# Rank 2 in place of rank 3 for the expert blocks of the second layer, in a one-core kernel of four gated layers

## The chip, the cores and the metric

The kernel runs on one core of one Trainium2 chip. The metric is device time in microseconds (us) from the first to the last instruction of the core; lower is better. A core has five engines that run side by side, each through its own list of instructions in order: PE (TensorE, matmuls), DVE (VectorE), ACT (ScalarE), POOL (GpSimd) and SP (SyncE, which here only issues transfers). They wait for each other by semaphores alone, so an instruction that waits holds up all that stand behind it on its engine.

## The reference

The input `x` has 32 sequences of 128 tokens with 128 features. It passes four layers, each a gated attention followed by a gated feed-forward part:

```python
x = x + tanh(g_xattn[0]) * L0_xattn(ctx, layernorm(x), b, seq_len)     # 16 heads
x = x + tanh(g_ffn[0])   * L0_ffn(layernorm(x), ...)                   # dense, 128 -> 512 -> 512 -> 512 -> 128
x = x + tanh(g_xattn[1]) * L1_xattn(layernorm(x), ctx, ...)            # 16 heads
x = x + tanh(g_ffn[1])   * L1_ffn(layernorm(x), ...)                   # see below
x = x + tanh(g_xattn[2]) * L2_xattn(ctx, layernorm(x), mask, b)        # 8 heads
x = x + tanh(g_ffn[2])   * L2_ffn(layernorm(x), ...)                   # 8 experts, top 2
x = x + tanh(g_xattn[3]) * L3_xattn(layernorm(x), ctx, ...)
x = x + tanh(g_ffn[3])   * L3_ffn(layernorm(x), ...)
```

The change lies in `L1_ffn` and in the attention behind it. `L1_ffn` is itself a causal attention with a mixture of experts behind it:

```python
h = rmsnorm(x, g1); c = h @ w_down
q, k, v = rope(c @ wq), rope(c @ wk), c @ wv           # 16 heads of 4
x = x + causal_softmax(q k^T / 2) v @ w_up
t = rmsnorm(x, g2); probs = softmax(t @ router_w)      # 8 experts
gate = the two largest probs of each token, scaled to sum 1
y = sum over experts of gate * (silu(t @ w1) * (t @ w3)) @ w2
```

## The kernel before

**A plan first, then five programs.** `make_plan` (from line 344 on) writes one long list of steps in Python. `run_program` then goes through that list once for each engine, and each engine emits its own part of every step. The order of the list is therefore the order of instructions on every engine. The plan keeps a clock for each engine with a reckoned cost for each kind of step (`reckon`), and uses it only to decide which piece comes next.

**Main work and side work.** An attention phase goes through 32 sequences (`b0` to `b31`). A step `scores` is a score tile for DVE to find row maxima in, `weights` is the transposed tile for ACT to take the exponential of, `sums` the product with the values. `weights` of a sequence come `lag` sequences after its `scores` (4 where there are 8 heads, 2 with 16). Everything else is side work: units with a need (semaphore counts that must be reached by the plan's clock) and a rank. `soon` puts a unit into the list `side` behind all units of the same or a lower rank number. `run_side(n, rank)` takes, up to n times, the first unit whose rank is at most `rank` and whose need is met. Between the units of an attention phase `go` calls `run_side(A.side, 2)` after each one, and `run_side(1)`, whose rank is 3, after every `A.every`-th one. For the causal attention `AF` (line 978 on, inside `L1_ffn`) that is two units of rank up to 2 behind every piece of main work, and one of rank up to 3 behind every second piece. For the third attention `A2` it is three and one, the latter behind every piece. `fill` calls `run_side(1)` where the plan finds PE waiting. `drain` runs side units until a condition holds. Rank 0 is an attention's own end work, rank 1 the preparation of later sequences, rank 2 the routing below.

**Routing and expert blocks.** When `AF` has finished four sequences (`f1_end`, DVE line 2139), `sorted_front` computes their routing as a chain of units of rank 2 (a *front*, numbered `g0` to `g7`): norm, transposes on PE, router product, exponential, ranking and picking on DVE (lines 2152 to 2199), places on PE and DVE (to line 2214, which writes `pidx`), then 8 scatters by POOL (line 2648), which put each token's row into the buffer `tok_rows` of its two experts. Four fronts make a half (h0: sequences 0 to 15; h1: 16 to 31). When a half is sorted, `blocks` can work through it: a table (DVE lines 2228 to 2253) and indices (2262 to 2267), then 24 blocks of 256 rows, `j0` to `j23`. A block is a load from `tok_rows` by SP, 2 transposes on PE and a copy of its weights on ACT, 8 matmuls (`block_up`), a tanh on ACT, two DVE operations (`block_gate`, lines 2272 and 2274), 8 matmuls (`block_down`), a copy on ACT and a store to `y_rows` by SP. The buffers of h0 carry the name `K`, those of h1 the name `KS`.

**The order around the change.** The blocks of h0 are added by `end1` when front g3 has finished, in the middle of `AF`. Behind `AF` stands `drain(lambda: not side)`: nothing of the next part begins until every side unit has been placed, and `after_f1 = now()` is what the next part waits for. Then POOL sets a part of `K8` to one (`k8_ones`, line 2642 on POOL, which waits for h0's last store), the blocks of h1 are added, the preparation of `A2` begins (`begin2`), and for each sequence POOL gathers its two expert results from `y_rows` (`fetch`, line 2654, two gathers each) and DVE adds them (`combine`, lines 2290 and 2292). `fetch` of sequence b needs the `combine` of b-8. After nine steps of `A2` a second drain waits until h1's blocks are stored; the next experts' weights are loaded then.

Of the kernel before, what the change touches and what calls it, by code (L numbers as in the profile page):

```python
# [185 lines left out]
class Plan:  # L186
# [65 lines left out]
    def dma(self, name, n=1):  # L252
        self.count[name] = self.count.get(name, 0) + 16 * n
        c = (name, self.count[name])
        self.at[c] = self.end + self.landing(name)
        self.fresh.append(c)
        self.made.append(c)
        return c
# [11 lines left out]
    def now(self):  # L270
        return tuple(self.last[n] for n in ("pe", "dve", "act", "pool") if self.last[n])
# [218 lines left out]
def make_plan():  # L490
# [11 lines left out]
    def soon(fn, need=(), rank=2, tag=None, unit=None):  # L502

        at_ = next((i for i, x in enumerate(side) if x.rank > rank), len(side))
        side.insert(at_, Step(fn=fn, need=need, rank=rank, tag=tag, unit=(unit or fn).__qualname__))
# [20 lines left out]
    def later():  # L526

        c = ("later", len(P.at))
        P.at[c] = P.clock["pe"] + 600
        return c  # L530
# [37 lines left out]
    def chain(fns, rank=2, tag=None):  # L568


        def part(i):
            return fns[i] if isinstance(fns[i], tuple) else (fns[i], None)

        def go(i):
            P.made = []
            if part(i)[0]() is False:
                soon(lambda: go(i), later(), rank, tag)
            elif i + 1 < len(fns):
                fn, need = part(i + 1)
                soon(lambda: go(i + 1), tuple(P.made) if need is None else need, rank, tag, fn)  # L580
            else:
                fns.append(None)
        soon(lambda: go(0), part(0)[1] or (), rank, tag, part(0)[0])
# [606 lines left out]
    def experts_of(i, **fields):  # L1190
        return Step(i=i, placed=0, scatters=[0, 0], scattered=[None] * 2, sorted=[None] * 2, xf_free=[None] * 2, t_free=[None] * 2, stored=[None] * 2, loaded=[None] * 2, done=[None] * 2, **fields)

    E1 = experts_of(0, gi=5, chunks=2, xf=(("HB", 6), ("HB", 7)), t=(0, 1), big="big_at0", weight="router_w", scale="g2", bcol=None, plus=None)
# [147 lines left out]
    t_m = dma("dma_moe1", 2)  # L1341
# [4 lines left out]

    def end1(h):
        if h == 0:
            chain(blocks(E1, 0, t_m, E1.begin, misc), 3)

    E1.end = end1
    run_f1()
# [1 line left out]
    after_f1 = now()  # L1354
# [42 lines left out]
    k8_free[:] = [after_f1] * 2 + [k8_ones[0]] * 2 + [k8_ones[1]] * 2  # L1397
    vr_free[:] = [after_f1] * 3
    pt_free[6:8] = E1.xf_free
    chain(blocks(E1, 1, t_m, after_f1, misc), 3)  # L1400
    begin2()
    chain([(lambda b=b: fetch1(b), lambda b=b: E1.stored[b // 16] or ()) for b in range(B)], 1)
    chain([(lambda b=b: add1(b), lambda b=b: got1.get(b, ())) for b in range(B)], 1)
# [1443 lines left out]
def build(nc, io, out, cu):  # L2847
    ctx = ExitStack()
    with ctx:  # L2849
        m = Memory(nc, ctx, io)  # L2850
        plan = make_plan()
        names = list(plan.count) + ["bias_parts", "lens", "vector_step", "pool_step"]
        sems = {n: ctx.enter_context(nc.semaphore(n)) for n in names}
        blk = ctx.enter_context(nc.Block())
        blk.sync(lambda e: sync_program(Engine(e, sems, None), plan, m, out))
        blk.tensor(lambda e: tensor_program(Engine(e, sems, None), plan, m))
        blk.vector(lambda e: vector_program(Engine(e, sems, "vector_step"), plan, m, cu))
        blk.scalar(lambda e: scalar_program(Engine(e, sems, None), plan, m))
        blk.gpsimd(lambda e: pool_program(Engine(e, sems, "pool_step"), plan, m))
# [65 lines left out]
```

How the kernel before makes its waits and increments, by code:

```python
    def wait_ge(self, *counts):  # L293
        for c in counts:
            if not c:
                continue
            if not isinstance(c[0], str):
                self.wait_ge(*c)
            elif self.passed.get(c[0], 0) < c[1]:
                self.passed[c[0]] = c[1]
                self.e.wait_ge(self.sems[c[0]], c[1])
# [1384 lines left out]
    def turn(u, src, n, need, ident, out=None):  # L1686
        pe.wait_ge(need, u.before)
        o = PSB[u.bank] if out is None else out
        for j in range(n):
            t = pe.e.transpose(o[:, 128 * j:128 * j + 128], src[:, 128 * j:128 * j + 128], ident)
        pe.done(t, u.full)
# [1 line left out]
    def setup(s):  # L1693
        pe.wait_ge(("bias_parts", 1), ("consts", 1))
        for i, u in enumerate(s.uses):
            if i:
                pe.wait_ge(("bias_parts", 2), u.before)
            t = pe.e.transpose(PSB[7].bitcast(BF16)[0:96, 128 * i:128 * i + 128], m.biasc[:, i, :], m.identb[:, :])
            pe.done(t, u.full)
# [1 line left out]
    def transpose_x(s):  # L1701
        pe.wait_ge(s.cst)
        turn(s.use, m.xn[:, s.k, :], s.n, s.need, C("ident"))
# [1 line left out]
    def scores(s):  # L1705
        A, p, b2 = s.A, s.b // 2, s.b % 2
        tiles = [m.K8] * A.ctx + [m.KS] * A.own
        out = PSB[s.use.bank]
        extra = A.bias_i is not None or A.causal
        pe.wait_ge(s.use.before, s.rows)
        for hh in range(A.per):
            h = s.i * A.per + hh
            for kb in range(A.nkb):
# [51 lines left out]
    def x1_v(s):  # L1765
        pe.wait_ge(s.need, s.use.before)
        for j in range(2):
```

## Time and profile before

| | us |
|---|---|
| median of 3 runs | 2389.68 |
| lowest and highest run | 2386.49, 2404.02 |
| profiled execution, time | 2409.28 |
| profiled execution, span of its trace | 2407.4 |

The profile is of one more execution, which took 2409.28 us: 19.6 us over the median of the runs, and 1.9 us of it lie outside its span. Over the span PE is busy 72%, DVE 57%, ACT 40% and POOL 31%, and the mean granted TensorE clock is 0.81 of full speed. PE's busy time is wall time: at the lower clock the same matmul counts for more. All times below are counted from the start of the span. A timeline row gives start and duration, and in brackets how long the engine had been idle and what ended that; a window row gives its length, then busy time with the number of instructions for each engine.

The parts of interest in the span: the causal attention `AF` ends at about 1384 us, the drain behind it at 1441 us, the first score tile of `A2` is read by DVE at 1526 us, and the last block of h1 is stored at about 1637 us.

### The profile page before, as it was taken

What the parts mean: (1) busy time and instruction counts of PE and PEld (TensorE: products, weight loads), DVE (VectorE), ACT (ScalarE), POOL (GpSimd) and SP (SyncE); (2) the same over time, 40 slices, a digit from 0 to 9 for tenths busy, and PEclk for the clock granted to TensorE, in tenths of its full rate; (3) what the DMA queues carried; (4) which work ended last, traced back from release to release, by engine and by line L of the source; (5) the groups of instructions that cost most, each with busy time, mean ns of one, the idle gap of its engine ahead of it and who ended that gap; (6) DMA issues with size and microseconds to landing.
All of it is one profiled execution on the core that took longest, in us unless ns stands there. A gap on an engine that the chain in (4) does not pass through costs nothing. (4 is left out here: it accounts for less than half of the span.)

```text
span 2407.4 us, 42348 instructions
## 1 busy us (share of the span) xinstructions
PE 1726.3 (72%) x14895; PEld 1218.7 (51%) x14902; DVE 1379.3 (57%) x4069; ACT 953.7 (40%) x1904; POOL 751.6 (31%) x1131
## 2 busy tenths in 40 slices
PE   2668879999688888898977874673681397874323
PEld 1335547667466666454544663552441386763211
DVE  4556664442477676475665445443864523658666
ACT  3335443333256665453433442341440264642112
POOL 4322100100522221234332116215516402253663
PEclk9868889999799888897888897786665598996555
DMA  6536555300255454221211122543530222120100
GB/s 176 119 78 125 105 178 156 70 1 1 44 113 103 92 99 77 87 49 46 52 48 52 40 66 66 124 105 125 121 71 32 78 64 69 63 71 27 35 27 9
DMA packets 189757, 184.46 MB, mean 77 GB/s; under 512 B 29509, under 2 KB 177925, under 8 KB 183557
## 3 DMA queue, kind: packets, MB, share of 16 engines
q1 hardware_dynamic: 180540, 145.04, 26.1%
q10 hardware_dynamic: 816, 19.92, 2.7%
q0 software_dynamic: 8192, 16.79, 2.4%
q8 instruction: 122, 2.00, 0.4%
q14 instruction: 87, 0.70, 0.1%
HBM read 119.47 MB, written 80.74 MB: 83 GB/s over the span
## 5 line engine op out<-in xcount | busy, mean ns | idle before, releaser
L2067 DVE TENSOR_REDUCE mneg<-psb 128x4 f32<-128x512 f32 (+1 forms) x576 | 386.6, 685 | 242.1 <-PE psb L1678 206.2
L2457 ACT ACTIVATE HB<-psb 128x512 f32<-128x512 f32 x384 | 222.3, 596 | 228.6 <-PE psb L1678 193.9
L1678 PE MATMUL psb<-K,Q 96*128 96x128 bf16 x1280 | 188.3, 249 | 66.2 <-DVE mneg L2067 27.2
L2677 POOL TENSOR_SCALAR rs<-mv 128x2 f32<-128x2 f32 (+1 forms) x96 | 22.7, 237 | 663.8 <-DVE mv L2027 655.3
L2457 ACT ACTIVATE HB<-psb,bias 128x512 f32<-128x512 f32 x192 | 131.5, 685 | 204.6 <-PE psb L1678 168.8
L1678 PE MATMUL psb<-Q,K 99*128 99x128 bf16 x1280 | 146.7, 246 | 88.3 <-DMA Q<-mT 87.1
L1678 PEld LDWEIGHTS psb<-K,Q 96*128 96x128 bf16 x1280 | 112.0, 111 | 122.5 <-issue 55.3
L1678 PEld LDWEIGHTS psb<-Q,K 99*128 99x128 bf16 x1280 | 108.6, 112 | 123.1 <-issue 108.4
L1678 PE MATMUL psb<-HB,VA 128*9 128x128 f32 (+1 forms) x2560 | 149.8, 313 | 13.0 <-issue 9.6
L1678 PE MATMUL psb<-KS,Q 96*128 96x128 bf16 x1024 | 150.0, 237 | 12.0 <-DVE mneg L2067 11.9
L1678 PE MATMUL psb<-K 128*128 128x256 f32 x576 | 152.7, 411 | 3.6 <-issue 2.6
L1678 PEld LDWEIGHTS psb<-K 128*128 128x128 f32 x576 | 113.1, 207 | 22.1 <-issue 6.6
L1678 PE MATMUL psb<-HB,VS 128*9 128x128 f32 (+1 forms) x2048 | 111.5, 293 | 7.8 <-ACT OE L2462 4.9
L1678 PE MATMUL psb<-Q,KS 99*128 99x128 bf16 x1024 | 110.3, 235 | 3.5 <-DMA Q<-mT 3.4
L1678 PE MATMUL psb<-cnegb,identb 128*128 128x512 bf16 x256 | 110.7, 433 | 0.0
L1678 PEld LDWEIGHTS psb<-KS,Q 96*128 96x128 bf16 x1024 | 91.3, 106 | 33.0 <-DVE mneg L2067 14.5
L1690 PE MATMUL psb<-cst,OE 128*128 128x128 f32 x480 | 98.0, 331 | 13.0 <-ACT OE L2462 6.3
L2284 DVE TENSOR_TENSOR K<-psb,HB 128x256 f32<-128x256 f32 x48 | 20.4, 424 | 141.6 <-PE psb L1678 115.8
L1678 PEld LDWEIGHTS psb<-WB,HB 128*128 128x128 f32 x768 | 95.4, 196 | 3.9 <-issue 1.2
L1678 PE MATMUL psb<-WB,HB 128*128 x768 | 95.2, 278 | 0.3 <-ACT HB L2542 0.3
L1678 PE MATMUL psb<-biasT,selbb 96*128 96x512 bf16 x192 | 92.9, 484 | 1.8 <-issue 1.8
L1678 PEld LDWEIGHTS psb<-Q,KS 99*128 99x128 bf16 x1024 | 80.9, 106 | 24.6 <-issue 14.3
(432 smaller groups left out, 4049.5 us busy)
## 6 DMA issues: line engine op xcount, KB each, us to landing
tok_rows<-in_zero ACTq DMA_DIRECT2D x16, 1152.0 KB, 31.1
K<-sc_k SPq DMA_DIRECT2D x32, 384.0 KB, 5.1
Q<-sc_q SPq DMA_DIRECT2D x32, 384.0 KB
sc_q<-comp SPq DMA_DIRECT2D x48, 192.0 KB, 2.2
K<-tok_rows SPq DMA_DIRECT2D x72, 128.0 KB
y_rows<-K SPq DMA_DIRECT2D x72, 128.0 KB
sc_q<-comp SPq DMA_DIRECT2D x48, 128.0 KB, 2.1
vraw<-in_ctx SPq DMA_DIRECT2D x48, 128.0 KB, 6.8
```

Of the source, the lines that this page charges most:

```text
L1678: return pe.e.matmul(out, w, x, start=start, stop=stop, skip_group_check=True)
L1690: t = pe.e.transpose(o[:, 128 * j:128 * j + 128], src[:, 128 * j:128 * j + 128], ident)
L2067: t = e.tensor_reduce(m.mneg[:, s.b % 4, s.i * A.per:(s.i + 1) * A.per], PSB[s.use.bank].rearrange("p (h k) -> p h k", h=A.per), AX.X, ALU ...
L2284: v.done(e.tensor_tensor(y2, o2, m.b2bc[:, bass.ds(at_, 128)].unsqueeze(1).broadcast_to([128, 2, 128]), ALU.add), s.use.drained)
L2457: a.done(act(m.HB[:, s.slot, :], PSB[s.use.bank], ACT.Exp, bias=bz), s.use.drained)
L2677: then(e.tensor_scalar(r0, var, EPS, None, ALU.add))
```

## The change

Both calls that add the blocks of the first experts pass rank 2 to `chain` in place of rank 3. Nothing else differs; the number of blocks and every instruction in them is the same.

```diff
     def end1(h):
         if h == 0:
-            chain(blocks(E1, 0, t_m, E1.begin, misc), 3)
+            chain(blocks(E1, 0, t_m, E1.begin, misc), 2)
...
     pt_free[6:8] = E1.xf_free
-    chain(blocks(E1, 1, t_m, after_f1, misc), 3)
+    chain(blocks(E1, 1, t_m, after_f1, misc), 2)
     begin2()
```

The plans agree up to front g4 and again from the tenth step of `A2` on; between them, 800 of 4596 steps, the order differs. Of the 24 blocks of h0, the plan before places 11 ahead of the end of sequence 31 and 13 behind it; the plan after places all 24 ahead of it. Three places show this.

DVE around the end of sequence 31 in `AF`, before. `U<-psb,U` is that end, `HB<-U,rs` and `LG<-psb` belong to front g7, and each pair of L2272 and L2274 is one block of h0:

```order
L2139 TENSOR_TENSOR U<-psb,U 128x128
L2024 BN_STATS st<-U 128x6 x4
L2027 BN_AGGR mv<-st 128x2 x4
L2272 SCALAR_TENSOR_TENSOR K<-K,psb 128x512
L2274 TENSOR_TENSOR K<-psb,K 128x512
L2042 TENSOR_SCALAR HB<-U,rs 128x128 x4
L2272 SCALAR_TENSOR_TENSOR K<-K,psb 128x512
L2274 TENSOR_TENSOR K<-psb,K 128x512
L2272 SCALAR_TENSOR_TENSOR K<-K,psb 128x512
L2274 TENSOR_TENSOR K<-psb,K 128x512
L2157 COPY LG<-psb 128x32
```

The same place on DVE after the change, from the last block of h0 on (`otmp` is the end work of sequences 30 and 31):

```order
L2272 SCALAR_TENSOR_TENSOR K<-K,psb 128x512
L2274 TENSOR_TENSOR K<-psb,K 128x512
L2090 RECIPROCAL rec<-psb 128x16
L2091 TENSOR_TENSOR otmp<-psb,rec 128x64
L2139 TENSOR_TENSOR U<-psb,U 128x128
L2090 RECIPROCAL rec<-psb 128x16
L2091 TENSOR_TENSOR otmp<-psb,rec 128x64
L2139 TENSOR_TENSOR U<-psb,U 128x128
L2024 BN_STATS st<-U 128x6 x4
L2027 BN_AGGR mv<-st 128x2 x4
L2042 TENSOR_SCALAR HB<-U,rs 128x128 x4
L2157 COPY LG<-psb 128x32
```

The pairs of blocks are gone from between the steps of front g7: behind sequence 31 the front stands alone.

DVE at the start of half h1, the difference (`-` before, `+` after). L2267 ends the indices, L2272 and L2274 are a block of h1, L2290 and L2292 a `combine`:

```order
 L2266 TENSOR_TENSOR KS<-KS,ek 128x32
 L2267 TENSOR_SCALAR pidx<-KS 128x2x16
-L2290 SCALAR_TENSOR_TENSOR U<-KS,gk,U 128x128 x2
-L2292 SCALAR_TENSOR_TENSOR X<-U,tg,X 128x128
+L2272 SCALAR_TENSOR_TENSOR KS<-KS,psb 128x512
+L2274 TENSOR_TENSOR KS<-psb,KS 128x512
 L2272 SCALAR_TENSOR_TENSOR KS<-KS,psb 128x512
 L2274 TENSOR_TENSOR KS<-psb,KS 128x512
 L2290 SCALAR_TENSOR_TENSOR U<-KS,gk,U 128x128 x2
 L2292 SCALAR_TENSOR_TENSOR X<-U,tg,X 128x128
```

The first `combine` stood ahead of the first block and now stands behind the second; on POOL the gathers of sequences 0 to 7 follow each other in both, and that of sequence 8 waits for the first `combine`.

SP where the first sequences of `A2` are stored and read back, the difference. `y_rows<-KS` is a block's store, `KS<-tok_rows` a block's load, `sc_q<-comp` the store of prepared queries:

```order
 L2726 DMA KS<-tok_rows 128x256
 L2726 DMA y_rows<-KS 128x256
-L2726 DMA sc_q<-comp 128x3x256
-L2726 DMA sc_q<-comp 128x2x256
-L2726 DMA sc_q<-comp 128x256
-L2726 DMA sc_q<-comp 128x3x256
-L2726 DMA sc_q<-comp 128x2x256
-L2726 DMA sc_q<-comp 128x256
```

Before, these six stores (sequences 0 to 3) came behind the store of block j6; after, the first three come behind that of j7 and the others behind that of j8. The first `scores` of `A2` stand behind 9 finished blocks before and behind 10 after, and the drain in `A2` holds 8 blocks before (j16 to j23) and 6 after (j18 to j23).

## Rows read from the trace of the kernel before

**Rows 1.** The page: span, PE's share, and one kind of store with its landing time.

```profile
span 2407.4 us, 42348 instructions
...
PE 1726.3 (72%) x14895; PEld 1218.7 (51%) x14902; DVE 1379.3 (57%) x4069; ACT 953.7 (40%) x1904; POOL 751.6 (31%) x1131
...
sc_q<-comp SPq DMA_DIRECT2D x48, 192.0 KB, 2.2
```

**Rows 2.** Windows: window, length, busy us (count) by engine, clock, DMA share, GB/s.

```profile
1290.00:1300.00 10.00, 10.00 (x91) 7.77 (x91) 6.64 (x19) 5.49 (x11) 0.00 (x0) 1.00 0.27 67
...
1360.00:1370.00 10.00, 5.21 (x60) 2.50 (x57) 0.62 (x2) 3.04 (x6) 7.02 (x8) 0.82 0.24 79
1410.00:1420.00 10.00, 5.03 (x32) 4.42 (x31) 2.76 (x4) 3.38 (x7) 5.75 (x6) 0.88 0.27 85
```

**Rows 3.** Windows: the drain behind AF, and all from the fourth front to its end.

```profile
1383.80:1440.90 57.10, 44.55 (x260) 38.70 (x260) 26.19 (x66) 25.83 (x53) 9.46 (x12) 0.94 0.21 68
...
1266.90:1440.90 174.00, 140.10 (x1093) 103.93 (x1090) 84.22 (x247) 76.56 (x159) 36.22 (x44) 0.89 0.18 54
```

**Rows 4.** Timeline of DVE: blocks of h0, end of sequence 31, front g7.

```profile
1293.43 0.69 DVE L2274 TENSOR_TENSOR K<-psb,K 128x512 f32<-128x512 f32 x1
...
1382.43 0.69 DVE L2274 TENSOR_TENSOR K<-psb,K 128x512 f32<-128x512 f32 x1
1383.79 0.29 DVE L2139 TENSOR_TENSOR U<-psb,U 128x128 f32<-128x128 f32 x1 [0.67 <-PE psb L1677]
...
1386.66 0.69 DVE L2274 TENSOR_TENSOR K<-psb,K 128x512 f32<-128x512 f32 x1
1387.58 0.88 DVE L2042 TENSOR_SCALAR HB<-U,rs 128x128 f32<-128x128 f32 x4 [0.22 <-POOL rs L2683]
...
1406.68 0.17 DVE L2214 CAST pidx<-pos 128x8 int32<-128x8 f32 x1
...
1438.41 0.69 DVE L2274 TENSOR_TENSOR K<-psb,K 128x512 f32<-128x512 f32 x1
1440.95 0.17 DVE L2228 TENSOR_TENSOR KS<-next,cst 128x8 f32<-128x8 f32 x1 [1.85 <-ACT K L2549]
```

**Rows 5.** Timeline of POOL: scatters of front g7, then gathers for sequences 0 to 11.

```profile
1407.63 1.09 POOL L2648 DMA_INDIRECT tok_rows<-HB,pidx  x1 [20.09 <-DVE pidx L2214]
...
1416.61 0.96 POOL L2648 DMA_INDIRECT tok_rows<-HB,pidx  x1 [0.30 <-issue]
1442.72 3.51 POOL L2642 MEMSET K<- 32x4096 bf16 x1 [25.15 <-DMA y_rows<-K]
1446.39 0.99 POOL L2654 DMA_INDIRECT KS<-y_rows,pidx  x1 [0.16 <-issue]
...
1477.10 0.94 POOL L2654 DMA_INDIRECT KS<-y_rows,pidx  x1 [0.30 <-issue]
```

**Rows 6.** Timeline of PE: front g7's transposes, and blocks of h0 and h1.

```profile
1390.90 0.63 PE L1690 MATMUL psb<-cst,HB 128*128 128x128 f32 x4 [0.57 <-ACT K L2549]
...
1435.92 1.97 PE L1678 MATMUL psb<-K 128*128 128x256 f32 x8
...
1453.04 3.75 PE L1678 MATMUL psb<-KS 128*128 128x256 f32 x8 [0.29 <-issue]
...
1479.58 0.66 PE L1690 MATMUL psb<-cst,KS 128*128 128x128 f32 x2 [19.00 <-issue]
```

**Rows 7.** Windows: h1 to the first scores of A2, nine steps of A2, second drain.

```profile
1440.90:1526.00 85.10, 42.50 (x183) 34.41 (x184) 41.50 (x116) 27.47 (x50) 44.18 (x57) 0.74 0.32 84
1526.00:1590.00 64.00, 45.72 (x319) 34.46 (x318) 33.28 (x96) 27.09 (x63) 18.37 (x40) 0.80 0.52 119
1590.00:1637.00 47.00, 32.78 (x201) 27.36 (x200) 22.07 (x66) 16.73 (x35) 6.97 (x10) 0.87 0.28 78
```

**Rows 8.** Timelines: SP's store of the first prepared queries, DVE's first maxima of A2.

```profile
1511.52 3.11 SPq L2726 DMA_DIRECT2D sc_q<-comp  x6
```

```profile
1526.22 0.69 DVE L2067 TENSOR_REDUCE mneg<-psb 128x4 f32<-128x512 f32 x1 [2.78 <-PE psb L1678]
```

## The prediction

> **What bounds the kernel now.** I read the page first: the span is 2407.4 us and PE is busy 72% of it [rows 1], the most of any engine, but a mean over very different parts. The change moves nothing outside the stretch from front g4 to the tenth step of `A2`, so I read that stretch in windows.
>
> Up to the end of `AF` PE is the limit wherever a block of h0 is at hand: in 1290 to 1300 it is busy all 10.00 us at full clock (1.00, the 2.4 GHz level) [rows 2]. The exception is POOL's runs of 8 scatters, one for each front. In 1360 to 1370 POOL is busy 7.02 us, PE only 5.21, DVE 0.62 and ACT 3.04; in 1410 to 1420 PE is busy 5.03 [rows 2]. Blocks were in the queues at both places, so this is not lack of work. I call such a run of indirect transfers a storm: while it lasts, the other engines come almost to a stop after its first few microseconds.
>
> From 1266.9 (front g4 about to scatter) to 1440.9 (end of the drain) there are 174.0 us, 140.1 of them PE busy, so 33.9 idle. The drain behind sequence 31, 1383.8 to 1440.9, holds 57.1 us with 44.55 busy, so 12.55 idle [rows 3]; the attention part keeps 21.35 idle. In the drain run 13 blocks of h0 (pairs of DVE from 1386.66 to 1438.41), the other 11 (1293.43 to 1382.43) lie ahead of it [rows 4]. The 13 take 44.55 / 13 = 3.43 us of PE each, front g7's small matmuls included.
>
> Behind 1440.9 PE isn't the limit. To the first scores of `A2` there are 85.1 us with 42.5 PE busy; then 64.0 with 45.72; then the second drain, 47.0 with 32.78 [rows 7]. The largest single hole is a storm of 24 gathers, 1446.39 to 1478.04 [rows 5]: PE stands 19.00 us until 1479.58 [rows 6].
>
> **The change, part 1: from front g4 to the table of h1.** All 13 blocks of the drain go ahead of the end of sequence 31. PE is full there, so they don't hide: the attention part grows by their PE time. What is left behind sequence 31 is front g7 alone, and its length is now what counts.
>
> That front ran among blocks: from 1384.08 (end of `U`) to 1406.85 (`pidx` written) it took 22.8 us [rows 4]. At its first handover to PE the input was ready at 1388.46 [rows 4] and the transposes began at 1390.90 [rows 6], 2.4 us late behind a block. There are four such handovers (transposes, router product, ranking behind the exponential, places). I take 2.15 us each, a little less than the one shown, so 8.6 in all, and get 14.2 us alone. Bounds: 13.2 (2.4 each) and 22.8 (nothing gained). Then 0.8 us to the first scatter, 10.0 us for eight (1407.63 to 1417.57) [rows 5], and the landing. No row has a scatter's landing; a store's median is 2.2 us [rows 1], I take 2.0. Sum 27.0 us, where 57.1 stood. About 1.5 us of PE work lies in it, so idle 25.5.
>
> With the work the same, the stretch is busy time plus idle time: before 140.1 + 21.35 + 12.55. After, 140.1 + 21.35 + 25.5, which is 187.0: **+13.0 us**. The three storms of g4 to g6 stay inside the attention. The fourth, of g7, now hits nobody, but its idle time is in the 25.5.
>
> Against that stands the clock. After a storm PE runs at the lower level for a while. The same 8 matmuls of a block take 1.97 us at full clock and 3.75 where the clock had fallen [rows 6]. Behind the storm of g7 some 4 us of matmuls ran slow; now none follow it but h1's, which start cold in both kernels. I take **-2 us**, between 0 and 10 (the whole stretch at full clock instead of 0.89 [rows 3] would make 140.1 about 130).
>
> The Trainium skill says the same of direction, and more of size: "TensorE: Matmul & The Clock Gate", Part 1 on the HAM clock gate, has a clock that is either full or half, so matmul time would double at most. By that rule the eight would take 3.94 us; the row shows 3.75, in agreement. The sum would be -2 by either.
>
> Part 1 is +11 us; bounds +3 (clock) and +20 (front g7 not faster).
>
> **Part 2: h1 and the start of A2.** Call the start of the table T (1440.95 before [rows 4]). Before, POOL waited for h0's last store, cleared `K8` from 1442.72 and gathered from T + 5.4 [rows 5]. Now h0 is stored long before; POOL clears directly behind the scatters (T - 2.0 to T + 1.5) and gathers from about T + 1.7. Sixteen gathers (sequences 0 to 7) at 1.26 us end at T + 21.9. The next waits for the first `combine`, which stands behind the second block on DVE. So the storm is cut there, where before it ran on through 24 to T + 37.1.
>
> Before, the engines went on for about 12 us into the storm, PE to 1460.57 (1479.58 less 19.00) [rows 6], 14 us behind 1446.39. The table and indices take T to T + 9, so by this row they get through before the stop. PE then resumes at about T + 23.5 in place of T + 38.6: **-15 us**. The gathers of sequences 8 to 15 follow in pairs among the blocks, 16 where before 8 remained. The price of 8 more I put at **+4 us**, of the size of the smallest stop seen (10.00 - 5.03 of PE [rows 2]), between 0 and 10.
>
> SP's first query store stands behind one block more (j7 for j6), in order, and everything from 1511.52 [rows 8] to the first maxima at 1526.22 [rows 8] hangs on it: one block, **+4 us** (3.43 plus its waits). The nine steps of `A2` hold one block more on a PE that is 71% busy [rows 7]: **+2**, between 0 and 3.4. The second drain holds 6 blocks for 8; at 47.0 / 8 = 5.9 us each the gain would be 12, but the queues' last work is fixed, so I take 4.5 each: **-9**.
>
> Part 2: -15 + 4 + 4 + 2 - 9 = -14 us; bounds -22 and 0. Behind the tenth step of `A2` the order is the same.
>
> **Sum.** +11 - 14 = -3 us. On the span, 2407.4 to 2404; on the median of the runs, 2389.7 to 2387. The profiled execution lies 19.6 us above the median, and I carry the difference over unscaled.
>
> **The rivals.**
> *The storm stops the table.* In the scatter storms the stop comes earlier than in the gather storm: by 1410 to 1420, two to three microseconds into the one that began at 1407.63, PE is already half idle [rows 2, 5]. If the gathers from T + 1.7 catch DVE inside the table, the rest of it runs at T + 23.5, h1's first block comes at T + 37 rather than T + 16, and the 15 us are gone along with the +4 for later pairs: +11 - 3 = +8, 2398. For it: DVE's table now lies in the storm, not ahead of it.
> The Trainium skill, "DMA: Bandwidth & Descriptors", section SWDGE vs HWDGE vs iDMA, speaks for no storm effect at all: software and hardware queues are different ones, and the DMA engine alternates between them. Then shortening a storm buys nothing and the sum would also be near +8. The rows above show engines stopping in storms, whatever the cause.
>
> *Slower: blocks hold PE in the attention.* PE takes its list in order. If a block's matmuls stand there before their load or DVE pair is ready, the attention waits too. The 13 moved blocks would then cost what blocks cost in the second drain, 5.9 us, not 3.43 [rows 7]: 13 x 2.5 = +32, total +29, 2419. It decides from (24 + 3) / 13 = 2.1 us of extra idle per block on. Against: 1290 to 1300 is full with blocks inside attention [rows 2].
>
> *Faster: blocks fill the attention's holes.* If the denser queue lets PE work on through the storms of g4 to g6, the 21.35 us go: -24, 2365. Against: blocks were queued in 1360 to 1370 and PE stood.
>
> **Chances.** Forecast 0.42; the storm stops the table, or storms don't matter, 0.30; slower by waiting blocks 0.15; faster by filled holes 0.13. A measurement here tells about 1% (24 us) from no change. The first two cases lie within it, so within 1% has 0.72, slower 0.15, faster 0.13. The range joins the bounds of both parts without letting all fall on one side: -20 to +21, 2370 to 2411. It leaves out most of the two outer rivals, but these have tails within it. The likeliest case's own range is 2378 to 2394.
>
> **What the profile will show.** If right: all 24 pairs of h0 ahead of the end of sequence 31, which comes 46 to 48 us later (1384 to about 1431); 25 to 29 us from it to the table with PE nearly idle; POOL's gathers beginning within 3 us of the table, a gap after the sixteenth; PE's stop ending near T + 24; the first maxima of `A2` near T + 78; h1 stored near T + 182. It is wrong if PE idles in the attention beyond the storms (third case), if the front takes over 33 us, or if DVE's table shows a hole of over 10 us (second case).

## The result, and the profile after

| | before | after |
|---|---|---|
| median, us (20 runs each, on one chip) | 2398.15 | 2408.81 |
| lowest and highest run | 2385.87, 2414.49 | 2396.40, 2428.92 |
| profiled execution, time | 2409.28 | 2397.88 |
| its span | 2407.4 | 2396.1 |

The ratio is 1.0044, 95% interval 1.0025 to 1.0062: slower, with 10.7 us between the medians. That is within the 1% called no change, and in the other direction than the forecast -3 us. The two profiled executions mislead: that of before lies 11 us above its median, that of after 11 us below. So I compared stretches between fixed points of the program, over several traces.

The page after, first: the same work, PE busy 71% of the span [rows 1].

```profile
span 2396.1 us, 42346 instructions
...
PE 1703.6 (71%) x14895; PEld 1206.3 (50%) x14902; DVE 1377.7 (57%) x4069; ACT 955.0 (40%) x1904; POOL 752.0 (31%) x1131
```

DVE around the end of sequence 31, after: the last block of h0 is done, then the front alone. Of the 24 pairs L2272/L2274 of h0 all stand ahead of 1417.36, where 13 stood behind [rows 4].

```profile
1407.96 0.69 DVE L2274 TENSOR_TENSOR K<-psb,K 128x512 f32<-128x512 f32 x1 [0.29 <-PE psb L1678]
...
1417.36 0.29 DVE L2139 TENSOR_TENSOR U<-psb,U 128x128 f32<-128x128 f32 x1 [1.24 <-PE psb L1677]
1421.17 0.88 DVE L2042 TENSOR_SCALAR HB<-U,rs 128x128 f32<-128x128 f32 x4 [2.10 <-POOL rs L2683]
...
1432.77 0.17 DVE L2214 CAST pidx<-pos 128x8 int32<-128x8 f32 x1
1445.02 0.17 DVE L2228 TENSOR_TENSOR KS<-next,cst 128x8 f32<-128x8 f32 x1 [12.07 <-DMA tok_rows<-HB,pidx]
```

POOL, after: the clearing of `K8` directly behind the last scatter, the first and sixteenth gather, and the wait of 6.07 us for the first `combine`. Before, the clearing waited 25.15 us for h0's last store and 24 gathers followed without a wait [rows 5].

```profile
1443.70 3.51 POOL L2642 MEMSET K<- 32x4096 bf16 x1
1447.37 0.99 POOL L2654 DMA_INDIRECT KS<-y_rows,pidx  x1 [0.16 <-issue]
...
1466.32 0.95 POOL L2654 DMA_INDIRECT KS<-y_rows,pidx  x1 [0.30 <-issue]
1473.33 0.94 POOL L2654 DMA_INDIRECT KS<-y_rows,pidx  x1 [6.07 <-DVE X L2292]
```

PE, after: the front's transposes, now at the low clock (1.12 us for four, 0.63 before [rows 6]), the first block of h1 behind 24.59 us without a matmul, and the two stops behind it (4.17 and 8.51) where one of 19.00 stood [rows 6]. The wait at the end is for the first prepared queries.

```profile
1422.10 1.12 PE L1690 MATMUL psb<-cst,HB 128*128 128x128 f32 x4 [4.78 <-DVE HB L2042]
...
1455.81 0.69 PE L1690 MATMUL psb<-cst,KS 128*128 128x128 f32 x2 [24.59 <-DMA KS<-tok_rows]
...
1471.00 0.66 PE L1690 MATMUL psb<-cst,KS 128*128 128x128 f32 x2 [4.17 <-ACT KS L2549]
...
1496.22 0.66 PE L1690 MATMUL psb<-cst,xn 128*128 128x128 f32 x2 [8.51 <-ACT KS L2549]
...
1523.25 0.58 PE L1678 MATMUL psb<-K,Q 96*128 96x128 bf16 x4 [5.88 <-DMA Q<-sc_q]
```

### The profile page after: what moved, and what is told of

The parts are those of the page before. It is cut to its first block and busy times, and to the rows that moved or that the text cites. A ratio compares the mean times of both kernels' runs of the same rounds, so it can differ in the third digit from the quotient of the medians.

```text
span 2396.1 us, 42346 instructions
## 1 busy us (share of the span) xinstructions
PE 1703.6 (71%) x14895; PEld 1206.3 (50%) x14902; DVE 1377.7 (57%) x4069; ACT 955.0 (40%) x1904; POOL 752.0 (31%) x1131
## 5 line engine op out<-in xcount | busy, mean ns | idle before, releaser
L1678 PEld LDWEIGHTS psb<-KS,Q 96*128 96x128 bf16 x1024 | 90.0, 105 | 27.2 <-issue 10.9
L2648 POOL DMA_INDIRECT tok_rows<-HB,pidx x64 | 62.6, 977 | 88.7 <-DVE pidx L2214 70.8
```

The source lines that it names most:

```text
L1678: return pe.e.matmul(out, w, x, start=start, stop=stop, skip_group_check=True)
L2648: e.indirect_dma_start(m.tok_rows, bass.IndirectOffsetOnAxis(ap=m.pidx[:, s.i, k, b:b + 1], axis=0), xf[:, 128 * s.j:128 * s.j + 128], Non ...
```

## The experiments

**What the stretches are.** Five points in DVE's timeline cut the stretch that changed: the places of front g3 (line 2214), the end of sequence 31, the table of h1 (line 2228), the first maxima of `A2` (line 2067), the last `block_gate` of h1 (line 2274), and behind them the places of the second front of the next experts (the point that one expectation calls the third front), from where the order is the same again. Some expectations count from the places of front g2 ("base"), 30 to 39 us ahead of g3's. The text ahead of the result has the order the same again from the tenth step of `A2`. DVE's list is the same again only from the 22nd score tile of `A2` (1672.3 us in the profile before, 1653.3 in the one after), two steps further.

**Each kernel again (r1, r2), and each edit alone (r3, r4).** All four ran on one chip.

> The kernel before, unchanged, for a second trace and for the size of the noise. Ratio 1.000 within 0.3%. If the trace of before shown so far was an unlucky one in h1's gathers (PE stood 19 us), this trace should show a shorter stop there: the two theories on where the 10.6 us lie differ in this. Theory A (the loss is PE work moved into the attention, and the start of h1 gives part of it back): from the first front to h1's table this trace is like the first one, and h1's stretch takes 196 us again. Theory B (the give-back seen in the first pair of traces is luck of one execution): h1's stretch takes 185 us or less.

> The changed kernel again, for a second trace: ratio 1.004 (1.002 to 1.007). Theory A: table of h1 about 27.5 us behind the end of sequence 31, and h1's stretch near 178 us as in the first trace. Theory B: h1's stretch takes 185 to 190 us.

Measured: r1 1.0004 (0.9975 to 1.0033), so the comparison finds nothing between equal kernels; r2 1.0007 (0.9984 to 1.0030), below what was expected of it. The change's loss was smaller here, and the intervals of the two measurements (this one and 1.0025 to 1.0062) barely overlap. The stretches were steadier than the medians, which the table further down shows: from the table to the last gate r1 takes 192.8 us (192.1 in the profile before) and r2 177.4 (174.2 in the one after). So the shorter second stretch was not luck of one execution, and theory A holds there.

```diff
 # r3: the first call alone; r4: the second call alone
-            chain(blocks(E1, 0, t_m, E1.begin, misc), 3)
+            chain(blocks(E1, 0, t_m, E1.begin, misc), 2)
```

> Rank 2 for the blocks of h0 alone. Theory A: nearly the whole effect, ratio 1.003 to 1.006, since all 24 blocks of h0 lie ahead of the end of sequence 31 as with the full change. A rival theory C (the loss comes from h1's blocks going ahead of the preparation of A2): ratio 1.000 or below.

> Rank 2 for the blocks of h1 alone; AF and its drain as before. Theory A: ratio 0.998 to 1.001 (one block more ahead of A2's first scores, two fewer in the second drain). Theory C: ratio 1.004 or more.

Measured: r3 1.0028 (1.0002 to 1.0054), with g2's places to the table 279.2 us and table to last gate 175.5: the changed kernel in every stretch up to there (the 163.3 us behind it, for 171 to 174, are given back later: from g2's places to the end of the span 1229.4 us, and 1230.1 in the profile after). r4 1.0037 (1.0014 to 1.0060), with 264.1 us to the table, as before, and then 200.3 to the last gate where before takes 190 to 193. So the first call does all that the changed kernel shows, and the lists say the same: on DVE r3 has the changed kernel's order up to 1622.5 us in the profile after, behind the last gate of h1. The second call alone costs some 8 us behind the table. Some 2.5 of them (88.1 to the first maxima, 85.6 before) lie where its lists are still those of before; the others, and the ratio of r4, are a cost that theory A (1.001 at most) did not foresee, and whose cause stays open. Theory C let the first call cost nothing, which r3 contradicts.

**Where the stretches stand.** The next jobs brought something that nothing in the kernels explains. The runs were made in groups (r1 to r4, r5 to r8, r9 to r12, r13 to r16, r17 and r18), which I call jobs. The kernel before had a median of 2398 to 2405 us in the comparison above and in the jobs of r1 to r4 and r9 to r12, and one of 2302 to 2308 us in those of r5 to r8, r13 to r16 and r17 to r18. It isn't the chip: r9 to r12 and r13 to r16 came from the same one. In the slower jobs PE stands 2.0 to 6.5 us of the 10 to 13 us of each run of 8 scatters, and in the gathers, as in the two profiles above. In the faster jobs it stands 0 to 2.1 us in the same runs, wherever it has work. I call them *with stops* and *without stops*, and compare only within one kind. Here are the DMA queues in 16 us of the same run of gathers, in the kernel before, with stops (r9, 1456 to 1472); columns are packets, MB and share of the 16 engines' time.

```profile
DMA packets 352, 0.72 MB, mean 45 GB/s; under 512 B 176, under 2 KB 176, under 8 KB 352
## 3 DMA queue, kind: packets, MB, share of 16 engines
q0 software_dynamic: 352, 0.72, 16.5%
```

The same stretch of it without stops (r17, 1387 to 1403):

```profile
q0 software_dynamic: 356, 0.74, 16.8%
q1 hardware_dynamic: 864, 0.79, 15.9%
q8 instruction: 1, 0.02, 0.5%
q14 instruction: 1, 0.01, 0.1%
```

POOL's queue moves the same in both. With stops nothing else moves in these 16 us, neither a block's loads and stores nor a packet of instructions, and the DMA engines are 83% idle meanwhile. That does not show a transfer held up by POOL's: SP issued none between its load at 1449.27 and its store at 1473.80, and the store stands behind a copy of ACT. ACT, and PE behind it, are what stood, and for ACT's 12.10 us the trace names no instruction of this core (r9):

```profile
1473.39 0.38 ACT L2549 ACTIVATE KS<-psb 128x256 f32<-128x256 f32 x1 [12.10 <-remote]
1473.92 0.66 PE L1690 MATMUL psb<-cst,KS 128*128 128x128 f32 x2 [17.58 <-ACT KS L2549]
```

In the first 8 us of the same run, in which SP's four loads were under way, 576 packets of the hardware queue moved with stops too. The Trainium skill, "DMA: Bandwidth & Descriptors", section SWDGE vs HWDGE vs iDMA, has the DMA engine alternate between the two kinds of queue. The traces without stops agree with that (356 packets of the one kind beside 864 of the other); those with stops don't speak against it, as no transfer of SP's was waiting in these 16 us. What stops the engines isn't known.

The windows of the kernel before with stops (r9), from g3's places to the last gate; columns as in [rows 2]:

```profile
1214.50:1381.90 167.40, 134.34 (x1199) 88.19 (x1197) 92.36 (x304) 67.45 (x145) 44.17 (x61) 0.85 0.16 46
1381.90:1436.80 54.90, 43.89 (x260) 38.02 (x260) 26.20 (x67) 25.87 (x53) 9.49 (x12) 0.97 0.22 71
1436.80:1521.00 84.20, 42.09 (x185) 34.02 (x186) 42.11 (x117) 27.51 (x50) 44.17 (x57) 0.74 0.31 82
1521.00:1626.40 105.40, 72.02 (x482) 56.89 (x481) 54.24 (x160) 42.50 (x94) 21.41 (x48) 0.83 0.45 106
```

The changed kernel with stops (the profile after):

```profile
1200.90:1417.40 216.50, 178.13 (x1421) 126.26 (x1419) 109.50 (x330) 91.99 (x195) 44.55 (x63) 0.87 0.17 52
1417.40:1445.00 27.60, 3.37 (x20) 2.79 (x20) 8.39 (x40) 4.56 (x3) 10.76 (x13) 0.51 0.06 19
1445.00:1524.30 79.30, 42.02 (x204) 34.52 (x205) 42.90 (x115) 26.09 (x53) 41.50 (x53) 0.78 0.33 89
1524.30:1619.20 94.90, 68.65 (x460) 54.64 (x459) 47.67 (x136) 40.90 (x89) 22.71 (x50) 0.86 0.47 114
```

The kernel before without stops (r17):

```profile
1181.70:1314.40 132.70, 120.96 (x1199) 81.58 (x1197) 92.08 (x305) 66.94 (x145) 44.14 (x62) 0.96 0.21 60
1314.40:1368.80 54.40, 44.07 (x260) 38.26 (x260) 26.16 (x67) 25.72 (x53) 9.45 (x12) 0.97 0.22 71
1368.80:1445.70 76.90, 44.68 (x186) 35.82 (x187) 42.04 (x117) 27.76 (x50) 44.25 (x57) 0.71 0.37 93
1445.70:1552.30 106.60, 76.39 (x483) 60.21 (x481) 53.27 (x161) 42.48 (x94) 22.41 (x47) 0.79 0.42 102
```

The changed kernel without stops (r15):

```profile
1184.50:1367.40 182.90, 163.16 (x1438) 118.55 (x1435) 109.41 (x329) 92.42 (x196) 44.06 (x62) 0.97 0.22 63
1367.40:1395.10 27.70, 3.38 (x21) 2.78 (x20) 8.43 (x41) 4.56 (x3) 10.77 (x13) 0.51 0.06 19
1395.10:1465.80 70.70, 41.52 (x203) 33.96 (x204) 42.45 (x114) 25.95 (x53) 41.55 (x53) 0.81 0.38 101
1465.80:1558.80 93.00, 69.65 (x461) 55.45 (x460) 47.44 (x137) 41.12 (x89) 22.75 (x50) 0.87 0.49 116
```

All traces of the two kernels together. With stops there are three of each (before: its profile, r1, r9; after: its profile, r2, r10) and the means stand here; without stops one of each, from the windows above, whose ends are rounded to 0.1 us.

| us | with stops: before | after | difference | without: before | after | difference |
|---|---|---|---|---|---|---|
| g3's places to end of sequence 31 | 167.3 | 218.7 | +51.4 | 132.7 | 182.9 | +50.2 |
| to the table of h1 | 56.2 | 27.7 | -28.5 | 54.4 | 27.7 | -26.7 |
| to the first maxima of `A2` | 85.6 | 80.8 | -4.8 | 76.9 | 70.7 | -6.2 |
| to the last gate of h1 | 105.9 | 94.7 | -11.2 | 106.6 | 93.0 | -13.6 |
| to the common order | 167.0 | 172.2 | +5.2 | 157.7 | 160.4 | +2.7 |
| sum | | | +12.1 | | | +6.4 |

The single values of a row lie within 2.5 us of its mean, the first and fifth row of before within 4. Other runs have the same lists in parts, and so more traces of these rows. Up to the table r4, r5, r11, r13, r14 and r18 are the kernel before, and r3 and r16 the changed one. With stops the first two rows then come to +50.1 and -28.5 (five traces of before, four of after), without stops to +50.6 and -25.3 (five and two): r17 had the second slowest of five stretches to the table, 54.4 where the others take 50.9 to 55.9. So the first two rows together are +21.6 to +22.9 us with stops and +23.5 to +25.3 without.

**Blocks held back for the front (r6, r8, r12).** The first chain in two pieces: rank 2 up to a block, rank 3 behind it.

```diff
-            chain(blocks(E1, 0, t_m, E1.begin, misc), 3)
+            units = blocks(E1, 0, t_m, E1.begin, misc)
+            chain([*units[:30], lambda: chain(units[30:], 3)], 2)   # r6; 22 in r8 and r12
```

> The first blocks' chain of h0 at rank 2 up to block j13 and at rank 3 behind it; h1 at rank 3. 19 blocks then stand ahead of the end of sequence 31 and 5 behind it, among the steps of front g7. Theory A (part 1 costs because front g7 stands alone, with idle time nobody fills): end of sequence 31 comes 8 x 3.43 = 27 us later than before, but from it to the table takes 31 rather than 57, so base to table is 261 to 264, as before, against 280 after the change; then 192 to the last gate as before, since the gathers still run 18 or more in a row; time within 0.2% of before. Theory B (moving a block into the attention costs by itself, whatever is left behind): base to table is longer by 8/13 of the 19 us, about 272, and the time about 12 us above before.

> The chain of h0 at rank 2 up to block j9 and at rank 3 behind it; h1 at rank 3. 16 blocks stand ahead of the end of sequence 31 and 8 behind it. Theory A: end of sequence 31 comes 5 x 3.43 = 17 us later than before, 40 us from it to the table, base to table 261 to 264, the rest and the time as before. Theory B: base to table longer by 5/13 of 19 us, about 268, time about 7 us above before.

> Rank 2 up to block j9 of h0 and rank 3 behind it, h1 at rank 3: 16 blocks ahead of the end of sequence 31, 8 behind it. The 8 are placed among the steps of front g7 (22.9 us to its places, as in the kernel before), so 35.1 us from the end of sequence 31 to the table. On a chip with stops: base to table 258 to 264, as before, time within 0.2% of before. Without stops: 217, within 3 us of before.

Measured: r6 1.0021 (0.9997 to 1.0044), r8 1.0015 (0.9996 to 1.0033), both without stops; r12 0.9994 (0.9968 to 1.0019), with stops. From g2's places to the table r6 took 228.8 us, r8 217.1, and r12 260.2; before takes 217.8 without stops (r17), and 264.1, 254.8 and 261.5 with them. (The other runs without stops that have before's list up to there take 214.5 to 219.4.) So theory A is right for 8 held blocks and wrong for 5, where theory B comes near (12 us foretold, 11 measured), and theory B is wrong for 8. The reason is in the windows from g3's places to the end of sequence 31, and from there to the table. First r8, 8 blocks held:

```profile
1187.70:1339.20 151.50, 138.23 (x1288) 96.18 (x1287) 98.53 (x313) 76.88 (x165) 44.05 (x61) 0.96 0.22 62
1339.20:1374.40 35.20, 28.70 (x170) 24.73 (x170) 19.32 (x57) 15.88 (x33) 9.49 (x12) 0.95 0.23 72
```

And r6, 5 blocks held:

```profile
1174.70:1336.80 162.10, 147.55 (x1343) 104.21 (x1341) 102.49 (x319) 82.92 (x177) 42.90 (x60) 0.96 0.22 61
1336.80:1372.00 35.20, 18.71 (x116) 16.39 (x116) 15.18 (x51) 13.49 (x22) 11.98 (x15) 0.80 0.17 57
```

Behind sequence 31 both take 35.2 us: with blocks in between, the front needs 22.9 us to its places and 12.3 more to the table, whether PE works (28.70) or not (18.71). Five blocks moved out of 13 shorten this stretch by 19.2 us (54.4 to 35.2) and lengthen the attention by 18.8 (132.7 to 151.5): no cost. The next three shorten nothing and cost 10.6. The last five shorten it by 7.5 (to 27.7) and cost 20.8 (162.1 to 182.9). With stops r12 says the same of the first five: 36.3 us behind sequence 31 (56.2 before, so -19.9) and 187.8 ahead of its end (168.0 as the mean of five traces, so +19.8). The whole loss of part 1 lies in the last eight. Eight blocks keep the front's stretch filled and five do not; 6 and 7 were not tried.

**Gathers 4 sequences ahead (r5, r7, r11, r14, r16).** One number in `fetch1` of the kernel before:

```diff
-        if E1.stored[b // 16] is None or b - 8 >= added1[0]:
+        if E1.stored[b // 16] is None or b - 4 >= added1[0]:
```

> The order of the kernel before, but the gathers of sequence b need the combine of b-4 in place of b-8 (the buffers are the same, so nothing new is awaited but the order of the list). Behind the table of h1 POOL's list then has the gathers of 4 sequences, the first combine, and pairs from there on, where 12 sequences' gathers (24) stood in a row. Theory A (the length of the unbroken run of gathers sets how long PE stands): PE's stop of 19 to 20.5 us shrinks to under 6, table to last gate of h1 goes from 192 to about 180, the stretch ahead of the table stays at 255 to 264, time about 10 us (0.4%) below before. Theory D (the run's length does not matter; h1 was shorter after the change because its gathers began earlier, beside the table): table to last gate stays at 190 to 194, time as before.

> The kernel before with the gathers of sequence b behind the combine of b-4 instead of b-8. On a chip with stops: PE's stop behind the table is under 6 us instead of 19 to 20.5, table to last gate about 180 instead of 192, time 10 us (0.4%) below before. Without stops: within 3 us of before in every stretch, so 0.1% or less; the 0.3% that the first look on such a chip gave would then be chance.

> The gathers of b behind the combine of b-4, once more. It measured 0.3% and 0.5% below before, with nothing gained between the table and the last gate (190.2, against 192.1, 192.8 and 189.7 before), 7 us gained between the last gate and the third front of the next experts, by one trace. If that is real it comes again: 158 to 163 there (163 to 170 before), time 0.3 to 0.5% below before. If not: time within 0.2%.

Measured: r5 0.9970 (0.9948 to 0.9991) and r14 0.9988 (0.9962 to 1.0013) without stops; r11 0.9947 (0.9919 to 0.9975) with them, so 2388.8 against 2402.1 us. The time fell as theory A said, but not where it said: from the table to the last gate r11 takes 190.2 us, as before, which is what theory D said, whose unchanged time was missed. PE in r11, behind the table at 1437.54:

```profile
1468.48 0.65 PE L1690 MATMUL psb<-cst,KS 128*128 128x128 f32 x2 [2.12 <-issue]
1477.26 0.66 PE L1690 MATMUL psb<-cst,KS 128*128 128x128 f32 x2 [4.07 <-ACT KS L2549]
...
1490.20 0.66 PE L1690 MATMUL psb<-cst,KS 128*128 128x128 f32 x2 [7.00 <-ACT KS L2549]
```

The stop of 19.00 is in pieces of 2 to 7 us, and the stretch from the table to the first maxima is 84.9 us, as before (84.2 to 87.4). What the stops cost in this stretch is the difference between the two kinds of job: 85.6 - 76.9 = 8.7 us before, 84.9 - 76.3 = 8.6 with 4 ahead, 80.8 - 70.7 = 10.1 after the change. With 24 gathers in a row, 10 and 16 these costs are nearly equal, so the length of the unbroken run doesn't set them in these three. Most of the gain of 4 ahead lies behind the last gate: 160.4 us to the common order with stops (167.0 before), 153.2 and 153.1 without (157.7); without stops the stretch from table to last gate is also shorter, 178.8 and 181.0 us against 183.5 in r17. Which wait became shorter there I did not find out.

> Both edits: 5 blocks of h0 held back for front g7, and gathers of b behind the combine of b-4. Theory A: base to table 261 to 264, table to last gate about 178, time 10 to 15 us (0.4 to 0.6%) below before. Theory B: base to table about 272, so the two edits cancel and the time is that of before. Theory D: as r6.

> The changed kernel with the gathers of b behind the combine of b-4. Base to table 279 to 285 (stops) as in the changed kernel. Behind it, if the gain of 4 sequences ahead does not depend on the rank of the blocks: 0.3 to 0.5% below the changed kernel, so within 0.2% of before. If both edits shorten the same run of gathers, so that the second finds nothing left: time as the changed kernel.

Measured, both without stops: r7 0.9992 (0.9968 to 1.0016), g2's places to the table 230.4 us, so 5 held blocks cost what 4 ahead gains. r16 1.0093 (1.0069 to 1.0118), where the changed kernel itself had 1.0071: 4 ahead gives the changed kernel nothing, as from the table to the first maxima it takes 79.6 us for 70.7, with two blocks more ahead of them.

**Gathers 2 sequences ahead (r13, r18).** The same line with `b - 2`.

> The kernel before with the gathers of sequence b behind the combine of b-2 instead of b-8. The first scores of A2 then stand behind 8 finished blocks of h1 and 8 combined sequences, the other 8 sequences are gathered in pairs beside the steps of A2. If only a long unbroken run stops PE: no stop over 3 us behind the first table, table to last gate about 178, time 15 to 20 us below before. If each gather costs what it costs wherever it stands (0.5 us of stopped PE each, 15 for 32): table to first maxima about 70, for the 2 blocks and 16 gathers that moved behind them, but first maxima to last gate longer by as much, table to last gate 188 to 192, time as with 4 sequences ahead.

> The kernel before with the gathers of b behind the combine of b-2. Without stops 0.1 to 0.4% below before, as in its first run. With stops: if what 4 ahead gained (0.5%) grows with the shortness of the run, 0.6 to 0.9% below before; if the number of gathers alone counts, 0.2 to 0.5%, no more than 4 ahead.

Measured, both without stops: 0.9977 (0.9959 to 0.9995) and 0.9974 (0.9957 to 0.9991). These two and r5 are below 1 with their whole interval where nothing stops, so 2 ahead beats both kernels there, and 4 ahead does with stops. What 2 ahead brings with stops was not measured, and so neither was the question whether each gather has its price. From the table to the first maxima it takes 61.5 and 61.3 us (76.9), to the last gate 172.6 and 174.1 in all (183.5), and it gives 11 to 13 us back up to the point of the common order (170.7 and 168.3, for 157.7). With 2 ahead DVE's list is before's only some 54 us further on, so the account can't be closed at that point; from the table to the end of the span it is 929.8 and 921.6 us for 935.2.

**The two kernels for their traces (r9, r10, r15, r17).**

> The kernel before once more, for a trace on the same chip as the next three. The first four runs came from one chip (kernel before 2405 us; PE stands 4 to 6 us in every run of 8 scatters and 19 to 20.5 us in the 24 gathers), the second four from another (kernel before 2308 us; PE stands 0 to 1.9 us in a run of scatters). Theory E (on one kind of chip the indirect transfers of POOL hold up everything else that moves, on the other they do not, and that is the whole 4% between them): if this chip shows the stops, base to table is 255 to 264 and table to last gate 192; if it does not, base to table is 213 to 216 and table to last gate about 180. Base is the writing of the places of front g2.

> The changed kernel once more. On a chip with stops: base to table 279 to 282, table to last gate 174 to 177, time 0.3 to 0.6% above before. On a chip without stops theory E says the change loses more: the front alone costs the same 27.7 us, so base to table grows by 24 us of idle time less the 6.3 that the drain had there, +18, and the shorter run of gathers gives nothing back: time 15 to 20 us (0.7 to 0.9%) above before. Rival F (what comes back behind the table comes from POOL's earlier start or from the order, not from shorter stops): the second stretch is 15 us shorter there too and the time 0.2 to 0.4% above before.

> The changed kernel. Where PE stands in the scatters (base to table 255 and more): time 0.3% above before, as so far. Where it does not: base to table 214.5 + 18 = 233 or more (idle time of the front alone 24.2 less the 8.7 that the drain had there, plus 13 blocks at 3.6 less the 42 they took in the drain), nothing back behind the table beyond the 5 us of the order, time 0.5 to 0.9% above before.

> The kernel before, for its trace. Without stops: base to table 214 to 217, table to first maxima 76 to 77, first maxima to last gate 102 to 106. Then what the changed kernel gets back behind the table (163.7) is 16 to 18 us with no stop to shorten, so it comes from the order alone. If instead table to last gate is 168 or less, nothing came back there and theory E stands. With stops: 255 to 264, 84 to 88, 105 to 107, as three times before.

Measured: r9 1.0017 (0.9987 to 1.0046) and r10 1.0026 (0.9999 to 1.0053), with stops; r15 1.0071 (1.0047 to 1.0095) and r17 0.9990 (0.9967 to 1.0014), without. So the change costs 0.1 to 0.4% with stops and 0.7% without. Theory E foretold r9's stretches with stops, but the stops don't belong to a kind of chip, and that they are the whole 4% wasn't shown. Its price for the changed kernel, 0.7 to 0.9%, was met, but not its reason: it let nothing come back behind the table beyond 5 us of the order, and in r15 19.8 us come back (163.7 for 183.5), more than with stops (16.0). That is what rival F said of the stretch; its time, 0.2 to 0.4% above before, was missed, because ahead of the table the changed kernel loses 23 us there.

## Why the prediction was wrong

**Front g7 alone: right.** 15.3 us from the end of sequence 31 to `pidx` (forecast 14.2), 27.7 to the table (27.0; told as 25 to 29), in all four traces of the changed kernel, with stops or without. The idle time behind sequence 31 is 24.3 us (25.5) for 12.0 as the mean of before.

**The 13 blocks in the attention: the step that failed.** The prediction let the attention grow by exactly their PE time, 13 x 3.43 = 44.6, with the idle time there unchanged, and then took 2 us off for the clock. Measured were +51.4 us with stops and +50.2 without. (What the profile was to show, an end 46 to 48 us later, does not follow from that sum, which gives 43 to 45.) With stops PE's busy time in the attention grew by 46.5 (132.1 to 178.6) and its idle time by 4.9; without stops busy by 42.2 and idle by 8.0. So the rival of the waiting blocks was there, at 0.4 to 0.6 us of extra idle time per block rather than the 2.1 from which it decides. What PE waited for shows it. Without stops, before (r17):

```profile
PE psb L1678 <- DVE mneg L2067: 8.6, 2, 8.4
PE psb L1690 <- ACT K L2549: 0.6, 1, 0.6
```

and after (r15), us in total, times, and the longest:

```profile
PE psb L1690 <- DMA K<-tok_rows: 4.9, 4, 3.1
PE psb L1678 <- DVE mneg L2067: 4.2, 1, 4.2
PE psb L1690 <- ACT K L2549: 3.4, 6, 0.6
PE psb L1729 <- ACT K L2549: 2.3, 4, 0.6
```

The waits for a block's load, and for ACT to copy a block's result out of its bank, grow from 1.1 to 11.5 us in all, with the short ones that are not shown (0.8 per moved block), and the wait for the attention's own row maxima shrinks by 4.4. One such load, in r15:

```profile
1257.92 0.44 PE L1690 MATMUL psb<-cst,K 128*128 128x128 f32 x2 [3.06 <-DMA K<-tok_rows]
```

**The clock: wrong sign.** Over attention and front, busy time rose by 5.8 us with stops (176.2 to 182.0) and by 1.5 without, where -2 was taken. (The single traces with stops have 172 to 178 before and 180 to 184 after.) The windows show one part: the front's matmuls, put at 1.5 us, take 3.37 at a clock of 0.51 (the 1.2 GHz level), after PE has stood in the front's waits. Without stops that is all of it. Where the rest comes from with stops I can't say.

Together part 1 is +22.9 us with stops and +23.5 without, not +11: idle time +17.1 and busy time +5.8 in the first case, 22.0 and 1.5 in the second, for forecast +13 and -2. Both lie above the stated bound of +20. So the terms that failed are the unchanged idle time in the attention (0 taken, +4.9 and +8.0 measured) and the clock (-2 taken, +5.8 and +1.5 of busy time measured); the idle time of the front alone was right.

**Part 2, its sum: close.** Forecast -14; the last three rows of the table give -10.8 with stops and -17.1 without. The signs foretold were there: gathers 2.3 us behind the table, a gap behind the sixteenth, the first maxima at T + 79.3 (78), the last gate at T + 174.2 and the last store issued at T + 176.8 (182 until it is stored).

**Part 2, its reason: wrong.** -15 us were to come from the shorter run of gathers. PE did come free at T + 26, but a second stop of 8.51 us and the wait for the queries took the gain back, and r15 with r17 show the same -6.2 up to the first maxima where there are no stops at all. The sum had -7 for that stretch (-15 + 4 + 4), and that the measured -4.8 and -6.2 lie near it is luck. What stays for it is that POOL begins its gathers 2.3 us behind the table and not 5.4, and the order; r6, which clears `K8` ahead of the table, has 70.1 us in that stretch, and r8, which clears it behind, 76.8. That is two kernels whose order differs in other places too, so this cause is argued, not shown. The terms +4 and +4 belonged to the same picture.

**The second drain.** Forecast +2 - 9 = -7 for the steps of `A2` and the drain. Measured -11.2 and -13.6 up to the last gate, of which +5.2 and +2.7 come back behind it: the first front of the next experts stood ahead of the last gate (its places at 1630.97 in the profile before, the gate at 1633.05) and now stands behind it (1653.27 and 1619.22). The forecast missed this move, since it took the order to be the same from the tenth step of `A2`. In sum -6.0 and -10.9.

**What stays open.** The ratios say +10.6, +1.7 and +6.2 us in three comparisons with stops, where the stretches say +12. Without stops they say +16, where the stretches say +6 and the one pair of traces has +3 ahead of them and +4 behind, in instructions that are the same. The difference of the two spans there, 13.5, is within the interval (11 to 22).

## What to carry to other kernels

Work that stands behind a long serial chain is its cover. Count first how much cover the chain needs: here 8 blocks of 13 filled a front's stretch of 35 us, five could be moved for nothing and the next eight cost 24 us. When a plan is changed by a rank, lay fixed points through several traces of each kernel and compare the stretches, as two single profiles said -11 us here where the medians said +11. And a stop that is seen in a trace is not yet a price: compare against a run in which it is missing.

## What the runs showed of the hardware

The same kernel took 2398 to 2405 us in some jobs and 2302 to 2308 in others, once both on the same chip. In the slower ones PE and ACT stood inside POOL's runs of indirect transfers, PE up to 20.5 us behind the table (r1), with no cause in the trace; in 16 us of one such run nothing but POOL's own packets moved, and SP issued nothing. In the faster ones PE, ACT and SP's transfers went on during the same runs. What sets it is outside the kernel, and open. From g3's places to the table of h1 the kernel before takes 223.4 us with stops and 187.1 without. These 36 us are more than a third of the whole difference; 25 of them are idle time of PE, and 11 are busy time, at a granted clock of 0.85 in the attention (r9) against 0.96 (r17).
